# A state-space scan on one Trainium2 core: states kept in PSUM, B dt x added by TensorE on padded 64-row halves

## The reference, cut to what matters

```python
xs = silu(x @ Win_x + bin_x);  z = x @ Win_z + bin_z
xp = xs @ Wx + bx                      # 16 columns for dt, 16 of B, 16 of C
delta = softplus(xp[..., :16] @ Wdt + bdt)
A = -exp(A_log)                        # 512 x 16
for t in range(64):                    # h: 32 x 512 x 16
    h = exp(delta[:, t] * A) * h + (delta[:, t] * xs[:, t]) * B[:, t]
    hidden[:, t] = sum over the 16 states of h * C[:, t]
out = ((hidden + xs * Dp) * silu(z)) @ Wout + bout
```

## Time and profile before

| what | value |
|---|---|
| time, median of 3 runs | 2482.11 us (2469.38 to 2485.14) |
| profiled execution, its own time | 2471.59 us |
| its span | 2469.8 us |
| granted TensorE clock over the span | 0.896 |
| `ssm_scan`, first POOL multiplication to last gate | 1690.5 to 2058.0 us |

### The profile page before, as it was taken

One profiled execution on the slowest core, in us unless ns is written; L12 is line 12 of the kernel. 1 busy time (PEld: TensorE's weight loads), 2 busy tenths in 40 slices (PEclk: granted clock), 3 DMA queues, 4 the chain that ended last, 5 costly groups with the idle time before them and its releaser, 6 DMA issues. The chain is left out here.

```text
span 2469.8 us, 65064 instructions
## 1 busy us (share of the span) xinstructions
PE 2260.2 (92%) x28672; PEld 1856.2 (75%) x28672; DVE 1538.0 (62%) x2661; ACT 1161.5 (47%) x1605; POOL 874.2 (35%) x637
## 2 busy tenths in 40 slices
PE   4899999999999999999999978967999999399994
PEld 2799999999999999999999966433444447399994
DVE  3555555555565555556555525185999985588885
ACT  2255555555555555555555542544444442166661
POOL 0222222222222222222212211136989882145551
PEclk9899999999999999999999999866665658599997
DMA  2111111111111111111111012004422220556664
GB/s 73 42 43 46 37 53 37 45 43 42 46 38 54 37 45 45 39 46 38 53 38 45 27 37 67 5 35 130 99 57 56 59 60 1 168 206 217 225 225 133
DMA packets 128333, 172.24 MB, mean 70 GB/s; under 512 B 17409, under 2 KB 108545, under 8 KB 127890
## 3 DMA queue, kind: packets, MB, share of 16 engines
q1 hardware_dynamic: 118242, 151.41, 20.5%
q0 software_dynamic: 4416, 12.06, 1.5%
q10 hardware_dynamic: 5392, 4.59, 0.6%
HBM read 128.05 MB, written 23.20 MB: 61 GB/s over the span
## 5 line engine op out<-in xcount | busy, mean ns | idle before, releaser
L497 DVE TENSOR_REDUCE max_part<-work 128x1 f32<-128x384 f32 (+1 forms) x1024 | 538.9, 569 | 240.2 <-PE work L625 216.6
L560 ACT ACTIVATE probs<-scores 128x1024 f32<-128x1024 f32 (+1 forms) x416 | 423.6, 1026 | 397.6 <-PE scores L650 383.7
L457 POOL TENSOR_TENSOR ctx_lo<-ctx_whole,ctx_hi 128x768 fp32r<-128x768 f32 (+1 forms) x128 | 231.9, 1811 | 1035.2 <-DVE ctx_hi L480 1003.9
L492 DVE SCALAR_TENSOR_TENSOR keys_lo<-work,bk,keys_hi 128x384 fp32r<-128x384 f32 (+1 forms) x256 | 162.5, 635 | 264.1 <-ACT keys_hi L539 264.1
L1154 POOL TENSOR_TENSOR xn_T<-delta_rep,xn 128x1024 f32<-128x1024 f32 x128 | 299.6, 2364 | 69.4 <-ACT xn L1171 37.0
L615 PE MATMUL work<-wv_hi,ctx_hi 128*128 128x256 f32 (+1 forms) x832 | 244.5, 294 | 2.0
L644 PE MATMUL scores<-q_hi,keys_hi 64*128 64x256 f32 (+1 forms) x1664 | 242.2, 283 | 0.0
L644 PE MATMUL scores<-q_lo,keys_hi 64*128 64x256 f32 (+1 forms) x1664 | 237.7, 277 | 0.0
L644 PE MATMUL scores<-q_hi,keys_lo 64*128 64x256 f32 (+1 forms) x1664 | 237.7, 277 | 0.0
L615 PE MATMUL work<-wv_hi,ctx_lo 128*128 128x256 f32 (+1 forms) x832 | 234.7, 282 | 0.0
L615 PE MATMUL work<-wv_lo,ctx_hi 128*128 128x256 f32 (+1 forms) x832 | 234.4, 282 | 0.0
(11 more groups left out here) (230 smaller groups left out, 4816.7 us busy)
## 6 DMA issues: line engine op xcount, KB each, us to landing
xs<-in_w_T SPq DMA_DIRECT2D x46, 1024.0 KB
ctx_whole<-in_ctx_T SPq DMA_DIRECT2D x96, 384.0 KB, 3.2
delta_rep<-delta SPq DMA_DIRECT2D x256, 64.0 KB, 2.0
ctx_whole<-in_ctx_T SPq DMA_DIRECT2D x32, 449.0 KB, 3.4
scratch_mixed<-mixed ACTq DMA_DIRECT2D x32, 128.0 KB, 1.8
mixed_b<-scratch_mixed SPq DMA_DIRECT2D x4, 1024.0 KB, 13.5
scratch_z<-z SPq DMA_DIRECT2D x16, 256.0 KB, 2.4
zg<-scratch_z SPq DMA_DIRECT2D x16, 256.0 KB, 3.2
```

What stands on the lines that cost most here:

```text
L457: nc.gpsimd.tensor_tensor(ctx_lo[c][:, :, 0:n], s.ctx_whole[c % 2][:, :, 0:n], ctx_hi[c][:, :, 0:n].bitcast(F32), ALU.subtract).then_inc(l ...
L492: nc.vector.scalar_tensor_tensor(keys_lo[par][:, m, start:start + n], bank[:, 0:n], s.bk[:, m:m + 1], keys_hi[par][:, m, start:start + n]. ...
L497: nc.vector.reduce_max(max_part[par][:, place(pair), c:c + 1], bank[:, 0:CHUNKS[c][1]], AX) \
L560: nc.scalar.activation(probs[slot][0:rows, :], scores[slot][0:rows, :], ACT.Exp, scale=1.0 / HD ** 0.5).then_inc(exp_done, 1)
```

## The change

- `delta` and `dtx` are written side by side into `s.steps`, and SP stores each tile of them (512 KB) to DRAM in `ssm_projections`. In the scan SP loads each step's 32 rows of both (4 KB per row) to all four quarters of `steps_in`, six steps ahead, released by `added`.
- The state of each half lives in PSUM (`state[i]`, two banks each). DVE multiplies it in place by `decay` (`keep`), the decays lying in a ring of four halves in SBUF: POOL writes delta * A there, ACT takes the exponential in place.
- B * dtx is added by PE: two float32 matmuls for each half (`add`), on rows 0 to 63 and 64 to 127, each of which holds B's diagonals in 32 rows and zeros in the other 32. Each goes to its own bank.
- ACT copies every half of the new state to SBUF (`copy`), into a ring of eight steps.
- The diagonals of B (two instructions a step) and of C (one) are made by DVE. Each multiplies 128 elements per partition, with both inputs in SBUF. POOL has the multiplication delta * A alone.
- The sum over states is made for four steps at a time, each step in its own 32 partitions (`sum_states`: one group of four steps per step of the loop), so that the tile of tokens comes out whole: DVE copies it (`copy_steps`), and `turn` transposes one block of 128 channels and adds its skip in each step.
- Step 0 needs no decay.

```diff
@@ ssm_projections, SyncE
+    for n in range(TT):
+        sp.wait_ge(dtx_done, n + 1)
+        sp.dma_start(of_steps(d)[n * P:(n + 1) * P, :], s.steps[:, n, :, :].rearrange("p i n -> p (i n)")) \
+            .then_inc(steps_stored, 16)
@@ ssm_scan
-REP, CS = 4, 4
+LOADS, DS, CS, BS, HS = 6, 4, 12, 3, 8
+b_of = [sb(f"b_of{i}", [P, NQ, STEPS]) for i in range(2)]
+a_wide = sb("a_wide", [P, NG, INNER])
+steps_in = [sb(f"steps_in{i}", [P, 2, INNER]) for i in range(LOADS)]
+b_diag = [[sb(f"b_diag{n}_{i}", [P, NQ, BATCH]) for i in range(2)] for n in range(BS)]
+decay = [sb(f"decay{i}", [P, 2, INNER]) for i in range(DS)]
+state = [ctx.enter_context(nc.psum_tensor(f"state{i}", [P, 2, INNER], F32)) for i in range(2)]
+y_steps = [ctx.enter_context(nc.psum_tensor(f"y_steps{i}", [P, INNER], F32)) for i in range(2)]
...
+    for t in range(STEPS):
+        if t >= LOADS:
+            sp.wait_ge(added, 2 * (t - LOADS) + 2)
+        rows = of_steps(d)[t * BATCH:(t + 1) * BATCH, :]
         for q in range(NQ):
+            sp.dma_start(steps_in[t % LOADS][BATCH * q:BATCH * (q + 1), :, :].rearrange("p i n -> p (i n)"),
+                         rows).then_inc(steps_loaded[t % LOADS], 16)
+        if t == 0:
+            for q in range(NQ):
+                sp.dma_start(c_of[BATCH * q:BATCH * (q + 1), :, :],
+                             d.bc[1].rearrange("(g q) (b t) -> q b g t", q=NQ, b=BATCH)[q]).then_inc(bc_loaded, 16)
+            sp.wait_ge(b_cleared, 2)
+            for g in range(NG):
+                first = 2 * BATCH * (g % 2)
+                sp.dma_start(b_of[g // 2][first:first + BATCH, :, :],
+                             d.bc[0].rearrange("(g q) (b t) -> g b q t", q=NQ, b=BATCH)[g]).then_inc(bc_loaded, 16)
...
+    for t in range(1, STEPS):
+        pool.wait_ge(steps_loaded[t % LOADS], 16 * NQ * (t // LOADS + 1))
         for i in range(2):
+            u = 2 * (t - 1) + i
+            if u >= DS:
+                pool.wait_ge(kept_done, u - DS + 1)
+            nc.gpsimd.tensor_tensor(decay[u % DS][:, :, :],
+                                    steps_in[t % LOADS][:, 0:1, :].to_broadcast([P, 2, INNER]),
+                                    a_rep[:, 2 * i:2 * i + 2, :], ALU.mult).then_inc(arg_done, 1)
...
+    def decays(t, i):
+        u = 2 * (t - 1) + i
+        act.wait_ge(arg_done, u + 1)
+        nc.scalar.activation(decay[u % DS][:, :, :], decay[u % DS][:, :, :], ACT.Exp, scale=-1.0) \
+            .then_inc(decay_done, 1)
+    def copy(t, i):
+        act.wait_ge(added, 2 * t + i + 1)
+        if t >= HS:
+            act.wait_ge(steps_summed, (t - HS) // TILE_STEPS + 1)
+        nc.scalar.copy(h[t % HS][:, 2 * i:2 * i + 2, :], state[i][:, :, :]).then_inc(h_copied, 1)
     act.wait_ge(a_made, NG)
+    decays(1, 0)
     for t in range(STEPS):
+        copy(t, 0)
+        if t + 1 < STEPS:
+            decays(t + 1, 1)
+        copy(t, 1)
+        if t + 2 < STEPS:
+            decays(t + 2, 0)
...
+    def diagonals(ring, of, t, done):
+        shape = [P, NG, BATCH]
+        nc.vector.tensor_tensor(ring[:, :, :], of[:, :, t:t + 1].to_broadcast(shape),
+                                same_batch[:, :].rearrange("p (a b) -> p a b", a=1).to_broadcast(shape),
+                                ALU.mult).then_inc(done, 1)
+    def b_diagonals(t, i):
+        if t >= BS:
+            dve.wait_ge(added, 2 * (t - BS) + i + 1)
+        diagonals(b_diag[t % BS][i], b_of[i], t, b_diag_done)
+    def c_diagonals(t):
+        if t >= CS:
+            dve.wait_ge(steps_summed, (t - CS) // TILE_STEPS + 1)
+        diagonals(c_diag[t % CS], c_of, t, c_diag_done)
+    def keep(t, i):
+        u = 2 * (t - 1) + i
+        dve.wait_ge(decay_done, u + 1)
+        dve.wait_ge(h_copied, 2 * (t - 1) + i + 1)
+        nc.vector.tensor_tensor(state[i][:, :, :], decay[u % DS][:, :, :], state[i][:, :, :], ALU.mult) \
+            .then_inc(kept_done, 1)
+    def copy_steps(n):
+        dve.wait_ge(steps_summed, n + 1)
+        if n >= 2:
+            dve.wait_ge(y_summed, n - 1)
+        nc.vector.tensor_copy(part[n % 2][:, :], y_steps[n % 2][:, :]).then_inc(steps_copied, 1)
...
+    for t in range(1, STEPS):
+        keep(t, 0)
+        if t + 1 < STEPS:
+            b_diagonals(t + 1, 0)
+        c_diagonals(t)
+        keep(t, 1)
+        if t + 1 < STEPS:
+            b_diagonals(t + 1, 1)
+        n, step = divmod(t, TILE_STEPS)
+        if n >= 2 and step == 0:
+            copy_steps(n - 2)
+        if n >= 3 and step == 1:
+            gate(n - 3)
+    gate(TT - 3)
+    copy_steps(TT - 2)
+    copy_steps(TT - 1)
+    gate(TT - 2)
     gate(TT - 1)
...
+    def add(t, i):
+        if t == 0:
+            pe.wait_ge(a_made, NG)
+        else:
+            pe.wait_ge(kept_done, 2 * (t - 1) + i + 1)
+        if i == 0:
+            pe.wait_ge(steps_loaded[t % LOADS], 16 * NQ * (t // LOADS + 1))
+        pe.wait_ge(b_diag_done, 2 * t + i + 1)
+        for j in range(2):
+            rows = slice(2 * BATCH * j, 2 * BATCH * (j + 1))
+            last = nc.tensor.matmul(state[i][:, j, :], b_diag[t % BS][i][rows, :, :].rearrange("p q b -> p (q b)"),
+                                    steps_in[t % LOADS][rows, 1, :], start=(t == 0), stop=True,
+                                    skip_group_check=True)
+        last.then_inc(added, 1)
+    def sum_states(n, g):
+        if g == 0:
+            pe.wait_ge(c_diag_done, TILE_STEPS * (n + 1))
             if n >= 2:
+                pe.wait_ge(steps_copied, n - 1)
+            pe.wait_ge(h_copied, 2 * TILE_STEPS * (n + 1))
+        for i in range(TILE_STEPS):
+            t = n * TILE_STEPS + i
+            last = nc.tensor.matmul(y_steps[n % 2][BATCH * i:BATCH * (i + 1), :], c_diag[t % CS][:, g, :],
+                                    h[t % HS][:, g, :], start=(g == 0), stop=(g == NG - 1),
+                                    skip_group_check=True)
+        if g == NG - 1:
+            last.then_inc(steps_summed, 1)
+    def turn(n, k):
+        if k == 0 and n >= 2:
+            pe.wait_ge(y_done, n - 1)
+        nc.tensor.matmul(y[n % 2][:, k, :], skip[:, k, :], s.xs[:, k, n * P:(n + 1) * P],
+                         start=(k == 0), stop=False, skip_group_check=True)
+        if k == 0:
+            pe.wait_ge(steps_copied, n + 1)
+        last = nc.tensor.matmul(y[n % 2][:, k, :], part[n % 2][:, k * P:(k + 1) * P], s.ident[:, :],
+                                start=False, stop=True, skip_group_check=True)
+        if k == KI - 1:
+            last.then_inc(y_summed, 1)
     pe.wait_ge(skip_made, KI)
     for t in range(STEPS):
+        add(t, 0)
+        add(t, 1)
+        n, step = divmod(t, TILE_STEPS)
+        if n >= 1:
+            sum_states(n - 1, step)
+        n, k = divmod(t - 1, TILE_STEPS)
+        if n >= 2:
+            turn(n - 2, k)
+    turn(TT - 3, KI - 1)
+    for g in range(NG):
+        sum_states(TT - 1, g)
+    for n in (TT - 2, TT - 1):
+        for k in range(KI):
+            turn(n, k)
```

More of the change, by code:

```diff
@@ L1007, in raw @@
                 act.wait_ge(filled, DT + n + 1)
-                nc.scalar.copy(s.dtx[:, n, :], banks[(DT + n) % BANKS][:, :]).then_inc(dt_raw, 1)
+                nc.scalar.copy(s.steps[:, n, 1, :], banks[(DT + n) % BANKS][:, :]).then_inc(dt_raw, 1)
             raw(0)
@@ L1033, in round_off @@
                 dve.wait_ge(dt_exp, n + 1)
[L1034 removed]
+                nc.vector.tensor_scalar(lost[n % RING][:, :], s.steps[:, n, 0, :], 1.0, -1.0, ALU.add, ALU.add) \
                     .then_inc(rounded, 1)
@@ L1140, in _ @@
                             .then_inc(x_turned, 16)
-                if t % TILE_STEPS == 0:
-                    load_z(t // TILE_STEPS)
+                if t % TILE_STEPS == 0 and t >= 5 * TILE_STEPS:
+                    load_z(t // TILE_STEPS - 3)
+            for n in range(TT - 3, TT):
+                load_z(n)
             sp.wait_ge(wout_loaded, 32)
@@ L1251, in sum_quarters @@
-            def sum_quarters(t):
-                pe.wait_ge(h_done, NG * (t + 1))
-                pe.wait_ge(c_diag_done, t + 1)
-                if t > 0:
-                    pe.wait_ge(parts_copied, t)
-                for g in range(NG):
-                    last = nc.tensor.matmul(y_parts[BATCH * g:BATCH * (g + 1), :], c_diag[t % CS][:, g, :],
-                                            h[t % 2][:, g, :], start=True, stop=True, skip_group_check=True)
-                last.then_inc(parts_done, 1)
@@ L1261, in sum_up @@
-            def sum_up(t):
-                n, step = divmod(t, TILE_STEPS)
-                if step == 0:
-                    if n >= 2:
-                        pe.wait_ge(y_done, n - 1)
-                    for k in range(KI):
-                        nc.tensor.matmul(y[n % 2][:, k, :], skip[:, k, :], s.xs[:, k, n * P:(n + 1) * P],
-                                         start=(k == 0), stop=False, skip_group_check=True)
-                pe.wait_ge(parts_copied, t + 1)
-                for k in range(KI):
```

(4 more changed lines are left out.)

163 lines of the change are left out of this document (46 added, 117 removed).

## The result

| | before | after |
|---|---|---|
| median of 5 runs | 2475.81 us (2469.38 to 2485.14) | 2499.73 us (2498.18 to 2502.49) |
| profiled execution | 2471.59 us | 2502.49 us |
| multiplication of half 0, step 1 / step 63 | 1699.98 / 2048.27 | 1698.49 / 2075.95 |
| one step, the difference over 62 | 5.62 us | 6.09 us |
| end of the last gate | 2057.99 | 2090.37 |

The ratio is 1.0094, 95% interval 1.0068 to 1.012: slower, by less than the 1% that I called the least change to tell. The forecast was 2530, 2.3% over the profiled run of before. Of the profiled runs' difference of 30.9 us the 62 steps hold 29.2, the end 4.7 and the start -1.5; the rest of the program takes back 1.5. By the medians the change is +23.9 us: the profiled execution of before lies 4.2 us under its median, that of after 2.8 us over.

What follows compares the result with a forecast made beforehand. It took PE at clock 0.50 to bound the old scan, at 5.62 us a step. With 6.4 us steps, 62 x (6.4 - 5.62) = +48 and +10 elsewhere on 2471.6 gave 2530 us, range 2440 to 2580.

Steps and rivals of the forecast that it cites:

- What bounds the kernel now: Old scan: PE without gaps at clock 0.50, 5.71 us a step; 5.62 over 62 steps; about 5.0 at full clock.
- The port: Scan: DVE diagonals with two SBUF inputs and POOL multiplications exclude each other whole, giving 6.3 us a step.
- One sign: Profile after: B diagonal of half 0, like the C diagonal, was to be above 1 us by its mean.
- a port that isn't contended: Rival, chance 0.15: short diagonals don't collide; 2420 at full clock with 4.7 us steps, 2545 at clock 0.50.
- DVE keeping the port over two diagonals: Rival, chance 0.10: only the two ends of POOL's instructions count; 5.3 us a step, 2457 us.
- the step length, 6.4 us: One scan step, taken between the port's 6.3 us and PE's 6.6 at clock 0.50; +48 us over 62 steps.
- the sum 0.16 + 2.34 + 0.16 + 1.12 + 0.19 + 2.34 = 6.3: Scan step in us: B diagonal half 0, POOL, C diagonal, `keep` of half 1, B diagonal half 1, POOL.
- The clock: PE's clock in the new scan, left open: PE work 6.6 us a step at 0.50, 3.6 at full clock.
- The ends: Outside the steady steps: +1 projections, -3 start, +4 first steps, +8 last sums and gate; together +10 us.
- The +4 for the first steps: First four or so scan steps: POOL's ring isn't full, every diagonal waits for a whole POOL instruction; +4 us.
- +58: Whole kernel: +48 us from 62 scan steps and +10 from the rest, on the profiled 2471.6 us.
- The halves run together: PE's `add` pairs on two row halves overlap: 1.9 us a pair at clock 0.50, 1.05 at full clock.

Runs made afterwards that it cites:

- e12: The kernel before, with delta x spread over all 128 rows by zero-padded selecting matrices instead of over 32 rows: 2440.55 us, ratio 0.9836.
- e1: The changed kernel with the diagonals' mask copied to PSUM, one bank for the token sums and their copy moved ahead of the diagonals: 2411.59 us.
- e7: The changed kernel with the additions reading only the 32 nonzero rows of each half: 2532.47 us, ratio to before 1.0216.
- e8: e1 with the additions reading only the 32 nonzero rows of each half: 2522.33 us.

## Why the prediction was right in sign and too large

**What bounds the kernel now** held, and e12 turned it round: with the clock at 0.82 instead of 0.59 the old step is 5.08 us.

**The port** held, step by step: C diagonal above 2 us, B half 0 at 1.34, B half 1 at 0.28 in the timeline, POOL's mean at 2.38. One sign just missed: by its mean B half 0 takes 0.98 us, not above 1; it lasts 0.37 to 1.47 us, and is shorter where DVE comes to it later, as behind the copy. The rivals are gone: a port that isn't contended would have given e1's 4.64 us in the kernel after; DVE keeping the port over two diagonals would have let the C diagonal follow B's at 1884.7.

**The step that failed is the step length, 6.4 us**, a term mis-sized twice. The first part is the sum 0.16 + 2.34 + 0.16 + 1.12 + 0.19 + 2.34 = 6.3. I charged POOL for every diagonal in its way. In the trace POOL's two multiplications with the diagonal between them last 4.72 us, where 4.64 was the pair with nothing between the earlier trace rows (I had 4.84); and B half 1 starts at 1888.13, before POOL's 1888.30, without holding it: where I had 0.19 for it stand the 0.08 in which POOL answers to `keep`. The C diagonal's end and `keep` together were right (0.07 + 1.22 for 0.16 + 1.12). 6.09 in all, 0.2 less, 13 us over 62 steps. The second part is the 0.1 that I added because I left the clock open: it stayed at 0.86, and PE did not bind (POOL waits for `keep` 60 times, 82.1 us, and for nothing else but the first load), 6 us.

**The clock** I left open although much hung on it, 33 us in this kernel (e7) and 111 us in e1 (e8): with 32 rows the time would have been 2532, near my 2530. The rows had it before me: 128-row work at 1.00, 17-row and 32-row work at 0.50 to 0.61.

**The ends.** Predicted +10: measured +4.7 at the end (14.4 us from the last `keep` of half 0 to the last gate's end, where I said 17.7 by +8) and -1.5 at the start, in which the later end of the block before is contained: the scan's loads begin at 1683.93 where they began at 1681.19, and the z stores stand behind the new ones. The rows are the first and last `keep` and the last gate, answering to the earlier trace rows:

```profile
1698.49 1.23 DVE L1244 TENSOR_TENSOR state<-decay,state 128x1024 f32<-128x1024 f32 x1 [6.47 <-ACT xn L1198]
...
2075.95 1.23 DVE L1244 TENSOR_TENSOR state<-decay,state 128x1024 f32<-128x1024 f32 x1 [0.91 <-ACT h L1198]
...
2089.68 0.69 DVE L1256 TENSOR_TENSOR xs<-y,zg 128x512 f32<-128x512 f32 x1 [1.09 <-PE y L1332]
```

The +4 for the first steps was too much: the first took 7.24 us, the next three 6.04 to 6.07, 1.1 us over the mean together. Of the 27 us between +58 and +30.9, the step's length holds 19 (62 x 0.31) and the ends and the rest of the program 8.

**The halves run together** (at full clock 1.13 us for an `add` pair, four matmul records, where the two of one matmul took 1.12), **the loads are hidden**, and `keep` into PSUM takes 1.22, inside its bounds.

The best version is e1, 2411.59 us, 2.8% faster than before and 88 us faster than the change as it was made: the plan with the states in PSUM was sound, and its diagonals stood in its way.

## What to carry to other kernels

When an engine beside GpSimd is to be busy all the time, count DVE's instructions with two SBUF inputs against the ends of GpSimd's instructions, and look at what stands behind each wait. Here two, each with its own end and slack behind it, cost 0.05 us each; three, two of them waiting in a row ahead of what GpSimd needed, cost 1.45 us. Putting a small constant operand in PSUM takes an instruction out of that count for one copy and room in a bank. Where TensorE at a low clock is the bound, matmuls on few rows are worth an attempt with zero rows added: the columns are the same, and here the granted clock went from 0.54 to 0.86 and from 0.59 to 0.82.

## What the runs showed of the hardware

- A DVE diagonal that slips between two POOL multiplications is all but free for POOL (4.72 us for the pair against 4.64), and may wait 2.43 us itself for 0.28 us of work; the record shows that wait as duration, not as idle time (its idle column says 0.0).
- In each of three pairs of kernels (e7 and after, e8 and e1, before and e12), whose matmuls differ only in the rows that some of them occupy, the granted clock is the higher with more rows: 0.54 and 0.86, 0.53 and 1.00 (1770 to 1970 us), 0.59 and 0.82. PE was busy 94% of e7's scan at 0.54, and 72% of that of after at 0.86.
